# Order of the products over pairs of accumulator banks in a split-precision graph layer

## The chip, the cores and the metric

The kernel runs on one core of a Trainium2 chip. The metric is the device time of one launch in microseconds, from the core's own clock; lower is better. In the text PE is the engine for matrix products, PEld its weight loads, DVE the vector engine, ACT the scalar engine, POOL and SP two further engines that here only issue transfers.

## The reference

`x` and the item features are 10000 x 128, `adj` is 10000 x 10000, all in 32-bit floats.

```python
h_user = max(layernorm(x), 0)
h = item_feat @ W_item.T + b_item
b = h_user @ W_user.T + b_user
out = x + relu(adj @ h + b)
```

Nearly all of the work is `adj @ h`.

## The kernel before

The output is kept turned: 128 features by 10000 users. The users are cut into five groups (`GROUPS`) of 2048 columns, and a group into four accumulator banks (`ACC_BANKS`) of 512 columns; the last group's fourth bank has only 272. Two sets of four banks take turns from group to group. The 10000 items are cut into 78 chunks (`CHUNKS`) of 128, and 16 left over. A tile is one chunk of one group: 128 items by 2048 users of `adj`, 1 MB. There are 5 x 78 = 390 tiles, and the order is all chunks of group 0, then all of group 1, and so on.

Products run in a rounded 32-bit format. To keep precision, each operand is split in two: the rounded value (`hi`) and the remainder (`lo`). Three products stand for one: `h_lo` times the rounded columns (L799), `h_hi` times the rounded columns (L800) and `h_hi` times the remainder columns (L806). So a tile takes 4 banks x 3 products = 12 products, each with its own weight load.

A tile passes through the engines like this. SP loads it into `a_ring` (eight slots; `load_tile`, L273) when the tile eight before it has been used. ACT rounds it into `hi_ring` (four slots; `round_hi`, L382) when the tile four before it has been used. DVE subtracts and writes the remainder over the tile's own slot, seen as `lo_ring` (`subtract_lo`, L496). In the first two tiles of the first group both steps are made in quarters, and in the next ten in halves (`parts_of`, L390 and L505), so that PE can start sooner. The semaphores `part_hi` and `hi_written` tell of rounded columns, `part_lo` and `lo_written` of remainders. PE's `tile` tells with `chunk_used` (on the last bank's remainder product) that both slots of the tile are free, and in a group's last tile with `acc_done` that a bank is complete. DVE then empties the banks (`empty`, L633), behind the subtractions of the second and third tile of the next group.

Between tiles PE's program places small products: those that make `h` from the items (`h_trio`, L725, in the first group), the mean and the variance of the layer norm (L744, L750), the user products (L758; L766, L767 and L769 from the second group on) and those of the left-over items (L780). All queues are written out by hand and run in program order. The last two tiles of the last group are issued apart: first three banks of both (`over=range(PARTS)`), then the fourth of both.

Of the kernel before, what the change touches and what calls it, by code (L numbers as in the profile page):

```python
# [35 lines left out]
ACC_BANKS = 4  # L36
BANK_PITCH = 512
SLOT_W = ACC_BANKS * BANK_PITCH
BANK_W = 512
# [10 lines left out]
CHUNKS = N_ITEM // P  # L50
# [3 lines left out]
PAIR = 2  # L54
# [26 lines left out]
PARTS = ACC_BANKS - 1  # L81
# [25 lines left out]
def unit_at(c, at, every):  # L107
    k, rest = divmod(c - at, every)
    return k if rest == 0 and 0 <= k < UNITS else None


def at_of(g, step):
    return (FIRST if g == 0 else LATER)[step]


def bank_w(g, k):
    return LAST_BANK_W if g == GROUPS - 1 and k == ACC_BANKS - 1 else BANK_W
# [6 lines left out]
def parts_of(g, c):  # L124
    if g > 0 or c >= QUARTERED + HALVED:
        return 1
    return ACC_BANKS if c < QUARTERED else ACC_BANKS // 2


def parts_before(c):  # L130
    return sum(parts_of(0, i) - 1 for i in range(c))
# [6 lines left out]
def graph_layer(nc, adj_tiles, adj_rem, item_t, x_slices, x_t, mean_of, w_item_and_bias, w_user_t, b_user, out_t):  # L138
    with ExitStack() as ctx:
        def sb(name, shape, dt=F32):  # L140
            return ctx.enter_context(nc.sbuf_tensor(name, shape, dt))

        def sem(name):
            return ctx.enter_context(nc.semaphore(name))
# [9 lines left out]
        hi_ring = sb("hi_ring", [P, S_SLOTS, SLOT_W], F32R)  # L154
        h_hi = sb("h_hi", [P, CHUNKS, HID], F32R)
        h_lo = sb("h_lo", [P, CHUNKS, HID], F32R)
        ring_at = nc.sbuf_base
        a_ring = sb("a_ring", [P, A_SLOTS, SLOT_W])
        lo_ring = nc.alloc_sbuf_tensor_at("lo_ring", [P, A_SLOTS, SLOT_W], F32R, offset=ring_at)
# [27 lines left out]
        def acc_of(g):  # L187
            return banks[g % 2]
# [16 lines left out]
        part_hi = sem("part_hi")  # L205
        part_lo = sem("part_lo")
# [25 lines left out]
        hi_written = sem("hi_written")  # L232
        lo_written = sem("lo_written")
        chunk_used = [sem(f"chunk_used{s}") for s in range(S_SLOTS)]
        acc_done = sem("acc_done")
        y_ready = [sem(f"y_ready{k}") for k in range(ACC_BANKS)]
# [468 lines left out]
        def _(pe):  # L705
# [78 lines left out]
            def tile(g, c, over=range(ACC_BANKS)):  # L784
                n, acc = g * CHUNKS + c, acc_of(g)
                s, r = n % A_SLOTS, n % S_SLOTS
                parts = parts_of(g, c)
                for k in over:
                    part, within = divmod(k, ACC_BANKS // parts)
                    if within == 0 and part < parts - 1:  # L790
                        pe.wait_ge(part_hi, parts_before(c) + part + 1)
                    elif within == 0:
                        pe.wait_ge(hi_written, n + 1)
                    if c == 0 and g > 1:

                        pe.wait_ge(y_ready[k], g - 1)
                    cols = slice(k * BANK_W, k * BANK_W + bank_w(g, k))
                    hi, lo = hi_ring[:, r, cols], lo_ring[:, s, cols]
                    nc.tensor.matmul(acc[k][:, 0:bank_w(g, k)], h_lo[:, c, :], hi, start=(c == 0), stop=False, skip_group_check=True)  # L799
                    nc.tensor.matmul(acc[k][:, 0:bank_w(g, k)], h_hi[:, c, :], hi, start=False, stop=False, skip_group_check=True)  # L800
                    if within == 0 and part < parts - 1:
                        pe.wait_ge(part_lo, parts_before(c) + part + 1)
                    elif within == 0:

                        pe.wait_ge(lo_written, n + 1)
                    last = nc.tensor.matmul(acc[k][:, 0:bank_w(g, k)], h_hi[:, c, :], lo, start=False, stop=(c == CHUNKS - 1),  # L806
                                            skip_group_check=True)
                    if k == PARTS:
                        last.then_inc(chunk_used[r], 1)
                    elif c == CHUNKS - 1:  # L810
                        last.then_inc(acc_done, 1)

            pe.wait_ge(warm_set, 1)
            warm(WARM_FIRST)
# [3 lines left out]
            for g in range(GROUPS):  # L818
# [4 lines left out]
                for c in range(CHUNKS):  # L823
                    if g == 0:
                        if c == 1:
                            h_trio(1)
                        if c in (TRIO, TRIO + 1):
                            h_trio(c - 1)
                        if c % PIECE_TILES == 0 and PIECE_TILES <= c < (PIECES - 1) * PIECE_TILES:
                            for part in range(PIECE_TRIOS):  # L830
                                h_trio(c // TRIO + LEAD + part)
                        if c == H_REM_AT:
                            h_rem_product()
                    if c == at_of(g, "mean"):
                        mean_product(g)
                    if c == at_of(g, "var"):
                        variance_product(g)
                    k = unit_at(c, at_of(g, "user"), NORM_EVERY)
                    if k is not None and g == 0:
                        user_product(g, k)  # L840
                    elif k is not None:
                        user_parts(g, k)
                    if c == at_of(g, "rem"):
                        left_over(g)
                    if g == 0 and c == 0:
                        pe.wait_ge(h_first_lo_set, 1)
                    elif g == 0 and (c == 1 or c % TRIO == 0):

                        pe.wait_ge(h_lo_set, c // TRIO + 1)
                    if g < GROUPS - 1 or c < CHUNKS - 2:  # L850
                        tile(g, c)
            for c in (CHUNKS - 2, CHUNKS - 1):
                tile(GROUPS - 1, c, range(PARTS))
            for c in (CHUNKS - 2, CHUNKS - 1):
                tile(GROUPS - 1, c, range(PARTS, ACC_BANKS))
# [40 lines left out]
```

## Time and profile before

| | |
|---|---|
| time, median of 3 runs (lowest to highest) | 1091.58 us (1090.75 to 1091.82) |
| the profiled execution's own time | 1091.69 us |
| its span, first to last instruction | 1089.9 us |
| PE busy | 1084.3 us (99%) |
| weight loads busy | 900.4 us (83%) |
| DVE busy | 989.0 us (91%) |
| ACT busy | 776.3 us (71%) |
| granted clock of PE, mean | 1.000 |
| read from memory | 417.04 MB, 387 GB/s over the span |

Busy means that the engine has at least one instruction in flight. On PE the instructions overlap: one starts before the one before it has ended, and its end in the trace is modelled. So a PE that is 99% busy can still run at different rates, and what counts is the step from one start to the next. The difference of 1.8 us between the execution's time and its span lies before the first instruction and after the last.

### The profile page before, as it was taken

The numbers are of one execution on the slowest core, as the hardware profiler recorded it, in microseconds if no ns is written. First come the engines' busy times: TensorE is split into PE (matmuls) and PEld (weight loads), VectorE is DVE, ScalarE is ACT, GpSimd is POOL, SyncE is SP. The second block draws the span as 40 slices with busy tenths as digits, with TensorE's granted clock in tenths as the row PEclk, the third lists the DMA queues.
The fourth block names the chain that finished last, engine by engine and source line by source line (L and its number), as shares of the span: only waits on it lengthen the run. The fifth ranks groups of instructions, "written<-read, shape, count | busy, mean of one in ns | idle before, by whom it ended". The sixth has DMA issues, their size and how long they took to land.

```text
span 1089.9 us, 12124 instructions
## 1 busy us (share of the span) xinstructions
PE 1084.3 (99%) x4956; PEld 900.4 (83%) x4956; DVE 989.0 (91%) x640; ACT 776.3 (71%) x492; POOL 33.7 (3%) x67
## 2 busy tenths in 40 slices
PE   9999999999999999999999999999999999999998
PEld 8888888788888888888888888888888888888887
DVE  6989999999899998898999988989999889899986
ACT  6767777667777776677777766777777667777763
POOL 0000000000000000000000000000000000000000
PEclk9999999999999999999999999999999999999999
DMA  9999999999999999999999999999999999999993
GB/s 388 416 425 406 424 425 398 341 370 416 415 395 395 395 401 380 377 414 404 397 391 400 391 379 368 424 395 385 423 397 378 379 358 414 378 408 406 380 353 134
DMA packets 65194, 422.99 MB, mean 388 GB/s; under 512 B 7977, under 2 KB 8778, under 8 KB 25202
## 3 DMA queue, kind: packets, MB, share of 16 engines
q1 hardware_dynamic: 60386, 407.61, 93.3%
q0 software_dynamic: 4608, 14.46, 4.2%
q8 instruction: 39, 0.64, 0.2%
q14 instruction: 17, 0.14, 0.0%
q10 hardware_dynamic: 144, 0.13, 0.0%
HBM read 417.04 MB, written 5.12 MB: 387 GB/s over the span
## 4 chain that ended last, share of the span: by engine, by line
PE 95%; DMA 2%; DVE 2%; ACT 0%; issue 0%; DVEq 0%; SPq 0%
PE acc L799 31%; PE acc L806 31%; PE acc L800 31%; DMA a_ring<-in_adj_tiles 2%; PE acc L725 1%; DVE lo_ring L496 1%; DVE lo_ring L505 0%; PE acc L766 0%; PE acc L769 0%; PE acc L767 0%; PE acc L758 0%; PE acc L780 0%; ACT hi_ring L390 0%; ACT hi_ring L382 0%; DVE y L633 0%
## 5 line engine op out<-in xcount | busy, mean ns | idle before, releaser
L382 ACT CAST hi_ring<-a_ring 128x2048 fp32r<-128x2048 f32 (+1 forms) x378 | 708.3, 1874 | 288.7 <-PE acc L806 265.1
L496 DVE TENSOR_TENSOR lo_ring<-a_ring,hi_ring 128x2048 fp32r<-128x2048 f32 (+1 forms) x378 | 841.1, 2234 | 80.0 <-ACT hi_ring L382 77.5
L799 PE MATMUL acc<-hi_ring,h_lo 128*128 128x512 f32 (+1 forms) x1560 | 602.9, 387 | 0.0
L806 PE MATMUL acc<-lo_ring,h_hi 128*128 128x512 f32 (+1 forms) x1560 | 599.8, 385 | 0.3 <-DVE lo_ring L505 0.2
L800 PE MATMUL acc<-hi_ring,h_hi 128*128 128x512 f32 (+1 forms) x1560 | 599.8, 384 | 0.0
L806 PEld LDWEIGHTS acc<-lo_ring,h_hi 128*128 128x128 f32 x1560 | 292.8, 188 | 60.4 <-DVE lo_ring L505 1.3
L799 PEld LDWEIGHTS acc<-hi_ring,h_lo 128*128 128x128 f32 x1560 | 292.9, 188 | 59.7 <-issue 2.7
L800 PEld LDWEIGHTS acc<-hi_ring,h_hi 128*128 128x128 f32 x1560 | 292.9, 188 | 58.0 <-issue 0.7
L505 DVE TENSOR_TENSOR lo_ring<-a_ring,hi_ring 128x1024 fp32r<-128x1024 f32 (+1 forms) x28 | 28.7, 1064 | 2.8 <-ACT hi_ring L390 2.6
L390 ACT CAST hi_ring<-a_ring 128x1024 fp32r<-128x1024 f32 (+1 forms) x28 | 24.5, 926 | 7.1 <-DMA a_ring<-in_adj_tiles 7.0
L326 POOL DMA_DIRECT2D y<-in_x_t x20 | 10.8, 542 | 529.3 <-ACT hi_ring L382 529.3
L725 PEld LDWEIGHTS acc<-wi_bi,items 128*128 128x128 f32 x156 | 20.3, 197 | 1.1
L725 PE MATMUL acc<-wi_bi,items 128*128 128x128 f32 x156 | 20.5, 280 | 0.0
L323 POOL DMA_DIRECT2D rows<-in_x_slices x20 | 10.9, 543 | 276.1 <-DVE normed_t L622 215.4
L633 DVE SCALAR_TENSOR_TENSOR y<-acc,y 128x512 f32<-128x512 f32 (+1 forms) x20 | 12.7, 671 | 4.2 <-PE acc L806 3.8
L526 DVE TENSOR_TENSOR h_full<-acc,wi_bi 128x384 f32<-128x384 f32 x25 | 13.7, 550 | 2.7 <-PE acc L725 2.7
L622 DVE STREAM_TRANSPOSE normed_t<-rows 128x512 f32<-128x512 f32 (+1 forms) x20 | 14.0, 700 | 0.7
L403 ACT CAST h_hi<-h_full 128x384 fp32r<-128x384 f32 x25 | 12.7, 507 | 1.4 <-DVE h_full L526 1.4
L537 DVE TENSOR_TENSOR h_lo<-h_full,h_hi 128x384 fp32r<-128x384 f32 x25 | 13.7, 548 | 0.0
L615 DVE SCALAR_TENSOR_TENSOR rows<-rows,stat 128x512 f32<-128x512 f32 (+1 forms) x20 | 13.4, 671 | 0.0
L583 DVE TENSOR_TENSOR rows<-rows,acc 128x512 f32<-128x512 f32 (+1 forms) x20 | 13.3, 666 | 0.0
L575 DVE TENSOR_REDUCE stat<-rows 128x16 f32<-128x512 f32 (+1 forms) x20 | 13.3, 666 | 0.0
(55 smaller groups left out, 155.6 us busy)
## 6 DMA issues: line engine op xcount, KB each, us to landing
a_ring<-in_adj_tiles SPq DMA_DIRECT2D x312, 1024.0 KB, 7.4
a_ring<-in_adj_tiles SPq DMA_DIRECT2D x78, 904.0 KB, 6.6
rows<-in_x_slices POOLq DMA_DIRECT2D x19, 256.0 KB, 7.0
y<-in_x_t POOLq DMA_DIRECT2D x19, 256.0 KB, 6.8
items<-in_item_t SPq DMA_DIRECT2D x12, 384.0 KB, 11.3
out_t<-y POOLq DMA_DIRECT2D x16, 256.0 KB, 7.1
a_rem<-in_adj_rem SPq DMA_DIRECT2D x20, 100.0 KB
out_t<-y SPq DMA_DIRECT2D x3, 256.0 KB, 2.7
```

The costliest lines, as they stand in the source:

```text
L382: nc.scalar.copy(hi_ring[:, n % S_SLOTS, cols], a_ring[:, n % A_SLOTS, cols]).then_inc(hi_written, 1)
L390: nc.scalar.copy(hi_ring[:, r, cols], a_ring[:, s, cols]).then_inc(part_hi if part < parts - 1 else hi_written, 1)
L496: nc.vector.tensor_tensor(lo_ring[:, s, cols], a_ring[:, s, cols], hi_ring[:, r, cols], ALU.subtract).then_inc(lo_written, 1)
L505: nc.vector.tensor_tensor(lo_ring[:, s, cols], a_ring[:, s, cols], hi_ring[:, r, cols], ALU.subtract).then_inc(part_lo if part < parts - 1 ...
L526: nc.vector.tensor_tensor(h_full[:, trio % H_BANKS, :, :], h_banks[trio % H_BANKS][:, 0:TRIO_W].rearrange("p (c d) -> p c d", d=HID), bi.u ...
L537: nc.vector.tensor_tensor(h_lo[:, trio * TRIO:(trio + 1) * TRIO, :], h_full[:, trio % H_BANKS, :, :], h_hi[:, trio * TRIO:(trio + 1) * TRI ...
L615: nc.vector.scalar_tensor_tensor(out=rows[:, b, :], in0=rows[:, b, :], scalar=0.0, in1=inv[:, b].unsqueeze(2).broadcast_to(wide(b)), op0=A ...
L622: nc.vector.transpose(normed_t[:, 0:n, :], rows[:, b, :]).then_inc(normed_t_ready, 1)
L725: last = nc.tensor.matmul(out, items[:, slot, at:at + P], wi, start=(m == 0 or (trio, m) == (0, 1)), stop=True, skip_group_check=True)
L799: nc.tensor.matmul(acc[k][:, 0:bank_w(g, k)], h_lo[:, c, :], hi, start=(c == 0), stop=False, skip_group_check=True)
L800: nc.tensor.matmul(acc[k][:, 0:bank_w(g, k)], h_hi[:, c, :], hi, start=False, stop=False, skip_group_check=True)
L806: last = nc.tensor.matmul(acc[k][:, 0:bank_w(g, k)], h_hi[:, c, :], lo, start=False, stop=(c == CHUNKS - 1), skip_group_check=True)
```

## The change

Only PE's `tile` changes. In a tile that covers all four banks, the banks are taken as two pairs, (0, 1) and (2, 3). In each pair first come the two products with rounded columns of the one bank and then those of the other, then the remainder product of the one and that of the other. A tile's order of products was, with A for L799, B for L800, C for L806: A0 B0 C0 A1 B1 C1 A2 B2 C2 A3 B3 C3. It becomes A0 B0 A1 B1 C0 C1 A2 B2 A3 B3 C2 C3. The waits stay with the products that need them. The two last tiles of the last group, which are issued by parts, keep the old order.

```diff
--- before.py
+++ after.py
@@ -785,30 +785,35 @@
                 n, acc = g * CHUNKS + c, acc_of(g)
                 s, r = n % A_SLOTS, n % S_SLOTS
                 parts = parts_of(g, c)
-                for k in over:
-                    part, within = divmod(k, ACC_BANKS // parts)
-                    if within == 0 and part < parts - 1:
-                        pe.wait_ge(part_hi, parts_before(c) + part + 1)
-                    elif within == 0:
-                        pe.wait_ge(hi_written, n + 1)
-                    if c == 0 and g > 1:
-
-                        pe.wait_ge(y_ready[k], g - 1)
-                    cols = slice(k * BANK_W, k * BANK_W + bank_w(g, k))
-                    hi, lo = hi_ring[:, r, cols], lo_ring[:, s, cols]
-                    nc.tensor.matmul(acc[k][:, 0:bank_w(g, k)], h_lo[:, c, :], hi, start=(c == 0), stop=False, skip_group_check=True)
-                    nc.tensor.matmul(acc[k][:, 0:bank_w(g, k)], h_hi[:, c, :], hi, start=False, stop=False, skip_group_check=True)
-                    if within == 0 and part < parts - 1:
-                        pe.wait_ge(part_lo, parts_before(c) + part + 1)
-                    elif within == 0:
-
-                        pe.wait_ge(lo_written, n + 1)
-                    last = nc.tensor.matmul(acc[k][:, 0:bank_w(g, k)], h_hi[:, c, :], lo, start=False, stop=(c == CHUNKS - 1),
-                                            skip_group_check=True)
-                    if k == PARTS:
-                        last.then_inc(chunk_used[r], 1)
-                    elif c == CHUNKS - 1:
-                        last.then_inc(acc_done, 1)
+                for pair in (over if len(over) < ACC_BANKS else range(0, ACC_BANKS, PAIR)):
+                    of_pair = (pair,) if len(over) < ACC_BANKS else (pair, pair + 1)
+                    for k in of_pair:
+                        part, within = divmod(k, ACC_BANKS // parts)
+                        if within == 0 and part < parts - 1:
+                            pe.wait_ge(part_hi, parts_before(c) + part + 1)
+                        elif within == 0:
+                            pe.wait_ge(hi_written, n + 1)
+                        if c == 0 and g > 1:
+
+                            pe.wait_ge(y_ready[k], g - 1)
+                        cols = slice(k * BANK_W, k * BANK_W + bank_w(g, k))
+                        hi, out = hi_ring[:, r, cols], acc[k][:, 0:bank_w(g, k)]
+                        nc.tensor.matmul(out, h_lo[:, c, :], hi, start=(c == 0), stop=False, skip_group_check=True)
+                        nc.tensor.matmul(out, h_hi[:, c, :], hi, start=False, stop=False, skip_group_check=True)
+                    for k in of_pair:
+                        part, within = divmod(k, ACC_BANKS // parts)
+                        if within == 0 and part < parts - 1:
+                            pe.wait_ge(part_lo, parts_before(c) + part + 1)
+                        elif within == 0:
+
+                            pe.wait_ge(lo_written, n + 1)
+                        cols = slice(k * BANK_W, k * BANK_W + bank_w(g, k))
+                        last = nc.tensor.matmul(acc[k][:, 0:bank_w(g, k)], h_hi[:, c, :], lo_ring[:, s, cols], start=False,
+                                                stop=(c == CHUNKS - 1), skip_group_check=True)
+                        if k == PARTS:
+                            last.then_inc(chunk_used[r], 1)
+                        elif c == CHUNKS - 1:
+                            last.then_inc(acc_done, 1)
 
             pe.wait_ge(warm_set, 1)
             warm(WARM_FIRST)
```

## Rows read from the trace of the kernel before

**Rows 1.** The page: span, and busy us (share) x instructions of each engine.

```profile
span 1089.9 us, 12124 instructions
...
PE 1084.3 (99%) x4956; PEld 900.4 (83%) x4956; DVE 989.0 (91%) x640; ACT 776.3 (71%) x492; POOL 33.7 (3%) x67
```

**Rows 2.** Chain of work that ended last, whole span: share by line.

```profile
PE acc L799 31%; PE acc L806 31%; PE acc L800 31%; DMA a_ring<-in_adj_tiles 2%; PE acc L725 1%; DVE lo_ring L496 1%; DVE lo_ring L505 0%; PE acc L766 0%; PE acc L769 0%; PE acc L767 0%; PE acc L758 0%; PE acc L780 0%; ACT hi_ring L390 0%; ACT hi_ring L382 0%; DVE y L633 0%
```

**Rows 3.** Timeline of PE, undisturbed stretch: start us, us, engine, line, operation.

```profile
519.65 0.39 PE L806 MATMUL acc<-lo_ring,h_hi 128*128 128x512 f32 x1
519.88 0.39 PE L799 MATMUL acc<-hi_ring,h_lo 128*128 128x512 f32 x1
520.11 0.39 PE L800 MATMUL acc<-hi_ring,h_hi 128*128 128x512 f32 x1
...
560.00 0.39 PE L799 MATMUL acc<-hi_ring,h_lo 128*128 128x512 f32 x1
```

**Rows 4.** Groups by form: xcount | busy us, mean ns | idle before.

```profile
L799 PE MATMUL acc<-hi_ring,h_lo 128*128 128x512 f32 x1482 | 580.8, 392 | 0.0
```

**Rows 5.** Waits, whole span: who waited for whom, us, times, longest.

```profile
ACT hi_ring L382 <- PE acc L806: 265.1, 337, 3.5
...
PEld acc L806 <- DVE lo_ring L505: 1.3, 3, 0.6
...
PEld acc L806 <- DVE lo_ring L496: 0.5, 1, 0.5
```

**Rows 6.** Timeline of PE, first and third tile of the first group.

```profile
9.79 0.39 PE L800 MATMUL acc<-hi_ring,h_hi 128*128 128x512 f32 x1
...
10.12 0.50 PE L806 MATMUL acc<-lo_ring,h_hi 128*128 128x512 f32 x1
...
14.13 0.39 PE L800 MATMUL acc<-hi_ring,h_hi 128*128 128x512 f32 x1
...
14.70 0.50 PE L806 MATMUL acc<-lo_ring,h_hi 128*128 128x512 f32 x1 [0.17 <-DVE lo_ring L505]
...
15.03 0.40 PE L799 MATMUL acc<-hi_ring,h_lo 128*128 128x512 f32 x1
```

**Rows 7.** Timeline near 89.93: DVE's subtraction and the products of bank 0 and 1.

```profile
87.60 2.27 DVE L496 TENSOR_TENSOR lo_ring<-a_ring,hi_ring 128x2048 fp32r<-128x2048 f32 x1
...
89.45 0.39 PE L800 MATMUL acc<-hi_ring,h_hi 128*128 128x512 f32 x1
...
89.93 0.50 PE L806 MATMUL acc<-lo_ring,h_hi 128*128 128x512 f32 x1
...
90.26 0.39 PE L799 MATMUL acc<-hi_ring,h_lo 128*128 128x512 f32 x1
```

**Rows 8.** Timeline of PE, last group: narrow bank, then the next tile.

```profile
1077.81 0.28 PE L799 MATMUL acc<-hi_ring,h_lo 128*128 128x272 f32 x1
...
1077.93 0.30 PE L800 MATMUL acc<-hi_ring,h_hi 128*128 128x272 f32 x1
...
1078.07 0.29 PE L806 MATMUL acc<-lo_ring,h_hi 128*128 128x272 f32 x1
...
1078.19 0.39 PE L799 MATMUL acc<-hi_ring,h_lo 128*128 128x512 f32 x1
```

**Rows 9.** Timeline at the first change of group: bank 0's last product, L633.

```profile
241.01 0.39 PE L806 MATMUL acc<-lo_ring,h_hi 128*128 128x512 f32 x1
...
241.51 0.69 DVE L633 SCALAR_TENSOR_TENSOR y<-acc,y 128x512 f32<-128x512 f32 x1
```

**Rows 10.** Timeline of PE behind the mean product, and the user products of group 1.

```profile
428.40 0.40 PE L766 MATMUL acc<-turned_hi,wu_lo 128*128 128x512 f32 x1
...
429.11 0.39 PE L799 MATMUL acc<-hi_ring,h_lo 128*128 128x512 f32 x1
...
501.02 0.39 PE L800 MATMUL acc<-hi_ring,h_hi 128*128 128x512 f32 x1
...
502.88 0.39 PE L799 MATMUL acc<-hi_ring,h_lo 128*128 128x512 f32 x1
```

## The prediction, made before the changed kernel had run

> **What bounds the kernel now.** I read the busy shares first, then the chain of work that ended last, then the waits, and last the timeline at the few places where the product engine is late. The shares say that PE has work in flight for 1084.3 of 1089.9 us and DVE for 91% [rows 1]. The chain says which of the two matters: the three product lines of `tile`, L799, L800 and L806, carry 31% of the span each, and the transfer of the matrix and the whole tiles' subtraction 2% and 1% [rows 2]. So the time is a number of products times the step from the start of one to the start of the next.
>
> That step is the quantity to know. Durations of products do not give it, because each is shown at 0.39 us and overlaps the next. In an undisturbed stretch the same instruction, L799, starts at 519.88 and again at 560.00 us, with 177 products from the one to the other (59 of each of the three lines): 40.12 us by 177 is 226.7 ns [rows 3]. Such products, 512 columns wide, number 3 x 1482 = 4446 [rows 4]; times 226.7 ns that is 1007.9 us of the 1089.9. The three kinds of step also look alike: from L806 to the next bank's L799 it is 0.23 us, and from there to L800, in the same bank, 0.23 us again [rows 3]. The engines that feed PE wait for it rather than the reverse: ACT stands 265.1 us for L806, while PE's weight loads stand 1.3 us and 0.5 us for the subtraction in the whole run [rows 5].
>
> **What the change can touch.** It adds and removes no instruction: 12 products and 12 weight loads per tile stay, and so do all increments. It moves four things.
>
> *The wait for the remainders.* In a whole tile the first product that reads them (call it C0) was third and becomes fifth. PE now stands there in few places. In the third tile C0 would follow L800 of 14.13 at 14.36 and starts at 14.70, 0.34 us late; the step behind it is 0.33 instead of 0.23 us, since the next weights had not been loaded ahead. That is 0.44 us in all [rows 6]. Two more products ahead of it are 2 x 0.227 = 0.45 us, so this stall should just vanish. At 89.93 the same happens: due at 89.68, 0.25 us late, and 0.10 us for the refill, 0.35 us [rows 7]. The subtraction that it waits for began at 87.60 at the end of an unbroken row of DVE work behind a late transfer, and does not come earlier when PE does. PE comes there 0.44 us earlier by the first gain and has its C0 0.45 us further back in the tile, so it arrives at about 89.69 and still stands until 89.93; but only 7 products of the tile are then left rather than 9. The two gains do not add: at this point the kernel is 0.45 us ahead, whatever it had won before. If the transfers behind that stretch, which are issued when PE frees a slot, also land earlier, both add up to 0.44 + 0.35 = 0.79 us. I take 0.45, because the chain there runs through DVE and the transfer, not through PE.
>
> *The waits of the quartered first two tiles.* There bank 1's rounded columns are now waited for ahead of bank 0's remainder product. The end of such a tile is its last remainder product in both orders: that one stands at 10.12, a step of 0.33 us after the preceding product instead of 0.23, in both versions [rows 6]. I put 0 on it; a cost of up to one refill, 0.1 us, is the bound.
>
> *The narrow bank of the last group.* Its fourth bank has 272 columns in 78 tiles, 76 of which take the new order (the last two are issued apart and keep the old one). Now the steps behind its three products are 0.12, 0.14 and 0.12 us [rows 8]: the second product in a row is the slower one. In the new order the two rounded products still follow each other, and the narrow remainder product stands by itself between wide ones. If the third then has the step of a first one, the gain is nearly 0 (0.12 against 0.12); if the 0.14 was the price of the remainder product's place, up to 76 x 0.02 = 1.5 us. The row of the first narrow product after a wide one (0.12) is nearest for the isolated product, and the 0.14 stays with the pair; a rounding of 0.01 leaves some 4 ns, 76 x 4 ns = 0.3 us. I take 0.3 us, with 0 and 1.5 as ends.
>
> *What leaves later.* The slot release (`chunk_used`) rides on bank 3's remainder product, the twelfth of the tile in both orders, so ACT's casts and SP's loads, which wait for it, move by nothing. In a group's last tile `acc_done` of banks 0 and 2 comes two products, 0.45 us, later. DVE's L633 waits for it with all later subtractions queued behind. At the first change of group bank 0's last product starts at 241.01 with a duration of 0.39, and L633 at 241.51 [rows 9]: 0.11 us of air, so DVE would stand about 0.34 us. DVE is by the program text working two tiles ahead there (L633 comes behind the subtraction of the next group's second tile), and with 91% busy it has time to spare [rows 1], so this costs nothing; without that cover it would be 4 x 0.34 = 1.4 us. POOL's stores of `y` start as much later; what POOL does next, the loads of x, waits for the cast of the group's 14th tile anyway.
>
> The sum is 0.45 + 0.3 = 0.75 us. The profiled execution took 1091.69 us, 0.11 above the median of 1091.58, and its span 1089.9; taking the gain from the median gives 1090.8 us. Less than 0.2% (2.2 us), about what a measurement of this kernel can tell from no change, is "within".
>
> **Does the step itself depend on the order?** This is the large unknown, as 1 ns on all products is 4.4 us. Two things are new. Steps to another bank rise from one in three to four in six. In the trace steps to another bank and within a bank are both 0.23 us [rows 3], so this gives 0. The Trainium skill, "Perfetto Trace Analysis", Matmul Optimizations, says otherwise: "Ensure all 8 PSUM banks are being leveraged to maximize available instruction-level parallelism." The trace does not agree, as far as its two kinds of step go. The second: two products in six now have another weight load beside them. The remainder weights `h_lo` load beside a rounded product, and `h_hi` beside a remainder product. No row of before shows these two combinations settled. The three that it shows all have the same step, and none of them is told apart by chunk or slot, so I take no change, with the nearest disturbed rows as bounds (below). The Trainium skill, "TensorE: Matmul & The Clock Gate", Step-by-step, has the weight load on a read port of its own that doesn't slow the running product; by it this term is nothing too, though the slower steps of [rows 10] are not explained by it.
>
> **Rivals.**
> - *Within 0.2%, and nothing gained* (1091.6 us): the stall at 89.93 is only moved and the narrow bank takes 4 ns less in no place. It differs from my forecast by 0.75 us and its sign can't be told from it.
> - *Faster, start-up.* All that PE stands for the subtraction goes, 1.3 + 0.5 = 1.8 us [rows 5] and four refills of 0.1, and some 0.7 us come at the narrow bank: 2.9 us, 1088.7 us. Against it: the stall at 10.12 sits at a tile's last product [rows 6].
> - *Faster, banks.* Steps to another bank get shorter. From 272 to 512 columns the step grows from 0.121 (my reading of 0.12 [rows 8]) to 0.2267, 0.44 ns a column, so 512 columns need 225.5 and 1.2 ns is what a step has beyond its columns. Gone from all 4446 that is 5.3 us, 1085.5 us. It is against the equal steps in [rows 3].
> - *Slower, weight loads.* The two new combinations run like the steps behind a disturbance: 8 steps from 501.02 to 502.88 take 1.86 us, 232.5 ns each, though weights and columns are the usual ones; with `wu` as weights, three steps from 428.40 to 429.11 take 0.71 us, 237 ns [rows 10]. On 1482 products that is 1482 x 5.8 ns = 8.6 us, 1099.4 us, or 1482 x 10 ns = 14.8 us, 1105.6 us. It decides from (0.75 + 2.2) / 1482 = 2.0 ns per product. For it: the step is plainly sensitive to something beside its width. Against: in undisturbed stretches it returns to 226.7 by itself.
>
> **How the numbers follow.** The forecast's own case gets 0.62, nothing gained 0.14; both end within 0.2%, 0.76. Faster start-up 0.06 and banks 0.05 make 0.11. Slower weight loads get 0.13. The first two hold 1090 to 1092 us and not quite 8 in 10; the range reaches to the start-up rival with 1 us of scatter, 1087.5, and to half the price of the weight loads, 1090.8 + 4.3 = 1095.1, rounded to 1095.0, because they may strike one combination of the two only.
>
> **What would show it.** L799 to L799 across an undisturbed stretch after: 226.7 ns per product if right, 228.7 or more if the weight-load rival decides. The wait of L806's weight load for the subtraction: one entry left near 90 us, that at 14.7 gone. The narrow steps: 0.14 only behind the second of the rounded pair. The prediction is wrong if the settled step moves by even half a nanosecond on average.

## The result, and the profile after

The changed kernel takes 1093.61 us (1093.24 to 1093.96), the kernel before beside it 1091.12 us (1090.73 to 1092.22). The ratio is 1.0022, 95% interval 1.0015 to 1.0030: 2.5 us slower, where 0.75 us faster was forecast. The profiled execution took 1093.24 us, its span is 1091.4 us.

The page of the changed kernel answers to [rows 1] and [rows 2]. L799, L800 and L806 are now L801, L802 and L811.

```profile
span 1091.4 us, 12124 instructions
...
PE 1086.7 (100%) x4956; PEld 900.3 (82%) x4956; DVE 989.1 (91%) x640; ACT 776.1 (71%) x492; POOL 33.7 (3%) x67
...
PE acc L801 32%; PE acc L811 32%; PE acc L802 32%; PE acc L725 2%; PE acc L710 0%; PE acc L766 0%; PE acc L769 0%; PE acc L767 0%; PE acc L758 0%; PE acc L780 0%; DVE y L633 0%; PE acc L744 0%; PE acc L750 0%; DVEq L139 0%; PE acc L733 0%
```

The same instructions, the same products on the chain, and the transfer and the subtraction have left the chain: by the summary alone this kernel looks better. Only PE's time is 2.4 us longer. The table of waits (who waited for whom: us, times, longest) shows less waiting too, against 1.3 and 0.5 us in [rows 5]:

```profile
PEld acc L811 <- DVE lo_ring L505: 0.9, 3, 0.5
...
PEld acc L811 <- DVE lo_ring L496: 0.3, 1, 0.3
```

So no wait that the profile shows makes the loss. To find where it is, I laid the start of the same product in both timelines side by side: the first product of a group, and of tiles far apart. First groups 1 to 3, from their first product to that of the last group, kernel before (start us, us, engine, line, operation):

```profile
243.28 0.39 PE L799 MATMUL acc<-hi_ring,h_lo 128*128 128x512 f32 x1
...
892.76 0.39 PE L799 MATMUL acc<-hi_ring,h_lo 128*128 128x512 f32 x1
```

and the changed kernel:

```profile
242.40 0.39 PE L801 MATMUL acc<-hi_ring,h_lo 128*128 128x512 f32 x1
...
891.88 0.39 PE L801 MATMUL acc<-hi_ring,h_lo 128*128 128x512 f32 x1
```

Both take 649.48 us for 234 tiles. The order in pairs costs and brings nothing there. Now 67 tiles of the last group, kernel before:

```profile
912.12 0.39 PE L799 MATMUL acc<-hi_ring,h_lo 128*128 128x512 f32 x1
...
1078.19 0.39 PE L799 MATMUL acc<-hi_ring,h_lo 128*128 128x512 f32 x1
```

and the changed kernel:

```profile
911.55 0.40 PE L801 MATMUL acc<-hi_ring,h_lo 128*128 128x512 f32 x1
...
1080.24 0.39 PE L801 MATMUL acc<-hi_ring,h_lo 128*128 128x512 f32 x1
```

166.07 us against 168.69 us: 2.62 us in 67 tiles, 39 ns a tile. From the head of the last group (892.76 and 891.88) to those last rows it is 185.43 against 188.36 us, 2.93 us. The whole difference of the two spans, 1.5 us, is then -0.88 us up to the end of group 0 (0.18 of it because the first product happened to start earlier, at 7.015 instead of 7.197), 0.00 in groups 1 to 3, +2.93 us in the last up to its 76th tile, and -0.5 us behind that. This last part is no gain of the change: from the start of the last product to the end it is 3.99 instead of 4.58 us, and in the traces of all kernels of this document this stretch takes 3.93 to 4.67 us in either order. The medians, without the luck of single executions, say 2.5 us: 2.9 lost and about half a microsecond won.

One tile of the last group in the changed kernel (the rows "x2" are two products, C0 with C1 or C2 with C3):

```profile
921.41 0.40 PE L801 MATMUL acc<-hi_ring,h_lo 128*128 128x512 f32 x1
921.64 0.39 PE L802 MATMUL acc<-hi_ring,h_hi 128*128 128x512 f32 x1
921.87 0.40 PE L801 MATMUL acc<-hi_ring,h_lo 128*128 128x512 f32 x1
922.11 0.39 PE L802 MATMUL acc<-hi_ring,h_hi 128*128 128x512 f32 x1
922.34 0.62 PE L811 MATMUL acc<-lo_ring,h_hi 128*128 128x512 f32 x2
922.80 0.39 PE L801 MATMUL acc<-hi_ring,h_lo 128*128 128x512 f32 x1
923.03 0.39 PE L802 MATMUL acc<-hi_ring,h_hi 128*128 128x512 f32 x1
923.25 0.28 PE L801 MATMUL acc<-hi_ring,h_lo 128*128 128x272 f32 x1
923.38 0.30 PE L802 MATMUL acc<-hi_ring,h_hi 128*128 128x272 f32 x1
923.51 0.53 PE L811 MATMUL acc<-lo_ring,h_hi 128*128 128x512 f32 x2
923.87 0.39 PE L801 MATMUL acc<-hi_ring,h_lo 128*128 128x512 f32 x1
```

The six wide products from 921.41 to 922.80 take 1.39 us, 232 ns each; six settled ones take 1.36. Starts are rounded to 0.01 us here. The differences of neighbouring starts in the trace's own nanoseconds show it better. `w` is the step behind a wide product, `n` behind a narrow one; the stretch begins behind 930 us in both:

```
before:  121n 134n 125n 227w 226w 227w 227w 226w 227w 227w 226w 227w | 121n 134n 125n 227w ...
changed: 232w 125n 125n 238w 124n 234w 231w 236w 228w 233w 230w 227w 227w 121n 134n
         233w 131n 229w 233w 236w 224w 231w 236w 228w 233w 125n 125n 237w 125n 234w ...
means over 50 us:  before  226.7 wide, 126.7 narrow;  changed  231.5 wide, 126.7 narrow
```

The narrow products are not slower in the mean. The wide ones behind them are, by 4.8 ns, nine to a tile: 43 ns. Over all 67 tiles it is 39 ns, because the small products between some tiles disturb the wide ones of the kernel before as well, and the changed kernel loses less there than elsewhere (2548 against 2533 ns in the tile behind the mean product). And they run in a row of steps that the kernel before knows as well: behind the mean product it shows 229, 234, 235, 225, 230, 236, 229, 232, 231 and then 227 ([rows 10] have the start of the first and of the ninth of these steps, 501.02 and 502.88). There it is paid once in a while, here in every tile.

### The profile page after: what moved, and what is told of

It is laid out like the page before. It is cut to its first block, busy times and chain, and to the rows that moved or that the text cites. A ratio compares the mean times of both kernels' runs of the same rounds, so it can differ in the third digit from the quotient of the medians.

```text
span 1091.4 us, 12124 instructions
## 1 busy us (share of the span) xinstructions
PE 1086.7 (100%) x4956; PEld 900.3 (82%) x4956; DVE 989.1 (91%) x640; ACT 776.1 (71%) x492; POOL 33.7 (3%) x67
## 4 chain that ended last, share of the span: by engine, by line
PE 99%; DVE 0%; issue 0%; DVEq 0%; POOL 0%; POOLq 0%
PE acc L801 32%; PE acc L811 32%; PE acc L802 32%; PE acc L725 2%; PE acc L710 0%; PE acc L766 0%; PE acc L769 0%; PE acc L767 0%; PE acc L758 0%; PE acc L780 0%; DVE y L633 0%; PE acc L744 0%; PE acc L750 0%; DVEq L139 0%; PE acc L733 0%
## 5 line engine op out<-in xcount | busy, mean ns | idle before, releaser
L801 PE MATMUL acc<-hi_ring,h_lo 128*128 128x512 f32 (+1 forms) x1560 | 604.0, 387 | 0.0
L802 PE MATMUL acc<-hi_ring,h_hi 128*128 128x512 f32 (+1 forms) x1560 | 597.3, 385 | 0.0
L811 PE MATMUL acc<-lo_ring,h_hi 128*128 128x512 f32 (+1 forms) x1560 | 475.2, 385 | 0.0
L801 PEld LDWEIGHTS acc<-hi_ring,h_lo 128*128 128x128 f32 x1560 | 292.9, 188 | 64.0 <-issue 2.7
L802 PEld LDWEIGHTS acc<-hi_ring,h_hi 128*128 128x128 f32 x1560 | 293.0, 188 | 59.0 <-issue 0.7
L811 PEld LDWEIGHTS acc<-lo_ring,h_hi 128*128 128x128 f32 x1560 | 288.2, 188 | 56.9 <-DVE lo_ring L505 0.9
L633 DVE SCALAR_TENSOR_TENSOR y<-acc,y 128x512 f32<-128x512 f32 (+1 forms) x20 | 12.7, 671 | 4.9 <-PE acc L811 4.4
```

The costliest lines, as they stand in the source:

```text
L801: nc.tensor.matmul(out, h_lo[:, c, :], hi, start=(c == 0), stop=False, skip_group_check=True)
L802: nc.tensor.matmul(out, h_hi[:, c, :], hi, start=False, stop=False, skip_group_check=True)
```

## The experiments

Tile times below are (start of a product in the 76th tile of the last group less that in the 9th) / 67; before 166.07 us / 67 = 2479 ns, changed 168.69 us / 67 = 2518 ns. They hold the user products and the like too, which are equal in all. All kernels that are compared were timed beside the kernel before.

**Where the loss is: pairs in all groups but the last, and in the last alone.** In the changed kernel:

```diff
-                for pair in (over if len(over) < ACC_BANKS else range(0, ACC_BANKS, PAIR)):
-                    of_pair = (pair,) if len(over) < ACC_BANKS else (pair, pair + 1)
+                single = len(over) < ACC_BANKS or g == GROUPS - 1
+                for pair in (over if single else range(0, ACC_BANKS, PAIR)):
+                    of_pair = (pair,) if single else (pair, pair + 1)
```

and for the second kernel `g < GROUPS - 1` instead of `g == GROUPS - 1`.

> The order in pairs in groups 0 to 3, the old order in the last group. Theory A (the loss is made in the last group, by a narrow remainder product of 272 columns standing alone between wide ones): the start-up gain of 0.7 to 0.9 us stays and the 3.0 us of the last group (76 tiles of 40 ns) go, so 1091.1 - 0.8 = 1090.3 us, and a tile of the last group takes 2.42 us as before. Theory B (the last group is slow because of a state that the pairs of groups 0 to 3 leave behind, in the slots or the queues): a tile of the last group still takes 2.46 us, 1093.6 us.

> The order in pairs in the last group alone. Theory A: no start-up gain, the whole loss, 1091.1 + 3.0 = 1094.1 us, a tile of the last group 2.46 us. Theory B: 1091.1 us, 2.42 us a tile.

Measured: without pairs in the last group 1090.93 us, ratio 0.9997 (0.9988 to 1.0006), 2479 ns a tile. With pairs there only, 1094.50 us, ratio 1.0029 (1.0018 to 1.0039), 2518 ns a tile, beside 1091.25 us for the kernel before. The rows of the second, as far apart as those above, 168.69 us again:

```profile
912.24 0.40 PE L802 MATMUL acc<-hi_ring,h_lo 128*128 128x512 f32 x1
...
1080.93 0.39 PE L802 MATMUL acc<-hi_ring,h_lo 128*128 128x512 f32 x1
```

The loss belongs to the last group's own order. Nothing is carried over from the groups ahead: theory B falls. The time without pairs in the last group can't be told from that of the kernel before, as the interval holds 1; that the start-up gain is there is seen in the traces (below), not in this time.

**Which part of the order: a pair of wide banks alone, and a pair with the narrow products kept together.** First, in the last group:

```diff
-                for pair in (over if len(over) < ACC_BANKS else range(0, ACC_BANKS, PAIR)):
-                    of_pair = (pair,) if len(over) < ACC_BANKS else (pair, pair + 1)
+                pairs = [(k,) for k in over] if len(over) < ACC_BANKS else [(0, 1), (2,), (3,)] if g == GROUPS - 1 else [(0, 1), (2, 3)]
+                for of_pair in pairs:
```

> Pairs everywhere, but in the last group only banks 0 and 1 are a pair; banks 2 and 3 (the narrow one) are taken one after the other. Theory A: the three narrow products stand together again, no loss, 1090.3 us, 2.42 us a tile. Theory C (any pair in a tile with a narrow bank is slow, since its first products still run behind the narrow ones): half of the loss or more stays, 1091.8 to 1093.3 us, 2.44 to 2.46 us a tile.

Then the pair of banks 2 and 3 again, but with C3 ahead of C2:

```diff
-                    for k in of_pair:
+                    narrow_first = g == GROUPS - 1 and of_pair == (2, 3)
+                    for k in (of_pair[::-1] if narrow_first else of_pair):
...
-                        if k == PARTS:
+                        if k == (2 if narrow_first else PARTS):
```

> Pairs everywhere, but in the last group's second pair the narrow remainder product comes ahead of the wide one: A2 B2 A3 B3 C3 C2. The order in pairs stays and the three narrow products stand together. Theory A: 1090.3 us, 2.42 us a tile. Theory D (it is the pairing of a narrow bank with a wide one, not the lone product): 1093.6 us, 2.46 us a tile.

Measured: 1090.73 us and 2479 ns a tile for the first (ratio 0.9996, 0.9987 to 1.0005), 1091.31 us and 2481 ns a tile for the second (1.0000, 0.9991 to 1.0008). Two tiles of the second, from head to head:

```profile
1058.09 0.39 PE L801 MATMUL acc<-hi_ring,h_lo 128*128 128x512 f32 x1
...
1060.51 0.39 PE L801 MATMUL acc<-hi_ring,h_lo 128*128 128x512 f32 x1
...
1061.87 0.39 PE L801 MATMUL acc<-hi_ring,h_lo 128*128 128x512 f32 x1
1062.10 0.39 PE L802 MATMUL acc<-hi_ring,h_hi 128*128 128x512 f32 x1
1062.32 0.28 PE L801 MATMUL acc<-hi_ring,h_lo 128*128 128x272 f32 x1
1062.44 0.30 PE L802 MATMUL acc<-hi_ring,h_hi 128*128 128x272 f32 x1
1062.58 0.51 PE L812 MATMUL acc<-lo_ring,h_hi 128*128 128x272 f32 x2
1062.93 0.39 PE L801 MATMUL acc<-hi_ring,h_lo 128*128 128x512 f32 x1
```

Each is 2.42 us long, with pairs in it. One exchange of two neighbouring products, C2 and C3, takes 37 of the 39 ns away. It is that the three narrow products are split, and not the pair: theory C falls on the first kernel, theory D on the second.

**Does it need pairs at all?** The kernel before, with only the last group's order written out. Three orders were run, the first of them:

```diff
+                if g == GROUPS - 1 and len(over) == ACC_BANKS:
...
+                    for what, k in [('A', 0), ('B', 0), ('C', 0), ('A', 3), ('A', 1), ('B', 1), ('C', 1), ('B', 3), ('A', 2), ('B', 2), ('C', 2), ('C', 3)]:
```

> The kernel before, and in the last group the three narrow products each stand alone, three wide ones apart, with no pair of wide banks: A0 B0 C0 A3 A1 B1 C1 B3 A2 B2 C2 C3. Theory S: every wide product runs in the slow sequence, at least 3 x (2 + 7 + 8) = 51 ns a tile and the narrow steps on top, 2.47 to 2.50 us a tile, 1095 to 1097 us. Theory P (a pair of banks is needed for the loss, the order by itself does nothing): 1091.2 us.

Measured: 1094.82 us, ratio 1.0031 (1.0020 to 1.0042), 2526 ns a tile, 47 ns more than before. Theory S expected at least 51 ns more and 1095 us, so both lie just below its range; theory P falls. No banks are paired there, and the loss is larger than the change's. In the rows each wide bank's three products stand between two narrow ones (the row "x2" is a wide bank's remainder product and the narrow one behind it):

```profile
961.02 0.39 PE L799 MATMUL acc<-hi_ring,h_lo 128*128 128x512 f32 x1
961.25 0.40 PE L799 MATMUL acc<-hi_ring,h_hi 128*128 128x512 f32 x1
961.49 0.52 PE L799 MATMUL acc<-lo_ring,h_hi 128*128 128x512 f32 x2
961.84 0.40 PE L799 MATMUL acc<-hi_ring,h_lo 128*128 128x512 f32 x1
962.08 0.39 PE L799 MATMUL acc<-hi_ring,h_hi 128*128 128x512 f32 x1
962.31 0.40 PE L799 MATMUL acc<-lo_ring,h_hi 128*128 128x512 f32 x1
```

In nanoseconds the steps are `123n 228w 235w 234w 130n 230w 233w 236w 119n 234w 231w 233w`, a mean of 232.8 for the wide ones. The narrow ones are even shorter than before, 125.0 in the mean.

The other two differ from it in the list alone: `A3 A0 B0 C0 A1 B1 C1 A2 B2 C2 B3 C3` and `A3 B3 C3 A0 B0 C0 A1 B1 C1 A2 B2 C2`.

> The kernel before, and in the last group one narrow product (bank 3's first) moved to the head of the tile's line: A3 A0 B0 C0 A1 B1 C1 A2 B2 C2 B3 C3. C3 of the tile before still stands ahead of A3, so the narrow products stand as B3 C3 A3, three together across the border of two tiles. No pairs anywhere. Theory S (each departure of narrow products from three together makes the wide ones behind it run through the same slow sequence, 229, 234, 235, 225, 230, 236, 229, 232 ns, 40 ns in all, until they settle at 226.7): nothing lost, 1091.2 us, 2.42 us a tile. Theory T (it matters which of the three products stand together and how weights and tiles change there): 1093 to 1094.2 us.

> The kernel before, and in the last group the whole narrow bank ahead of the wide ones: A3 B3 C3 A0 B0 C0 and so on. Theory S: the three stay together, nothing lost, 1091.2 us, 2.42 us a tile. If the place in the tile counts (the wide bank 0 directly behind it): up to 1094 us.

Measured: 1092.08 us (1.0006, 0.9997 to 1.0015) and 2483 ns a tile for the first, and 1091.56 us (1.0000, 0.9991 to 1.0009) and 2479 ns for the second. The narrow bank may thus stand first in the tile as well as last. The first kernel shows more. Its first tile opens with A3 alone, with nothing narrow ahead of it. The first fifteen tiles of its last group then last 2.47 us each (without the mean product at the end of the fifteenth), though from the second on the three narrow products follow each other. Behind that product and one more tile they settle at 2.42 us, in the same order of products. One stretch from C3 to C3 of each kind:

```profile
904.82 0.29 PE L799 MATMUL acc<-lo_ring,h_hi 128*128 128x272 f32 x1
...
907.29 0.29 PE L799 MATMUL acc<-lo_ring,h_hi 128*128 128x272 f32 x1
...
934.58 0.30 PE L799 MATMUL acc<-lo_ring,h_hi 128*128 128x272 f32 x1
...
937.00 0.30 PE L799 MATMUL acc<-lo_ring,h_hi 128*128 128x272 f32 x1
```

In nanoseconds a tile has the steps `129n 238w 229w 234w 235w 225w 230w 236w 229w 232w 125n 125n` in the first stretch and `125n 227w 227w 226w 227w 227w 226w 227w 227w 226w 121n 134n` in the second. Fifteen times 47 ns is 0.70 us, and from the head of the group to its 76th tile this kernel takes 186.11 us against 185.43 before: 0.68 of the 1.0 us by which its median is higher. So three narrow products together cost nothing if the wide ones ahead of them have settled. If these still run in the slow row, the row can start anew behind them, tile after tile, as it did here until the mean product. Theory S holds only with this condition, and theory T falls, since the same three products stand together in both stretches.

**Is it the width?** In the kernel before and in the changed one the narrow bank was made wider, the further columns being zeros of padding:

```diff
-LAST_BANK_W = N_USER - (GROUPS * ACC_BANKS - 1) * BANK_W
+LAST_BANK_W = 480
```

> The kernel before with the last bank of the last group 480 columns wide in place of 272 (the further columns are zeros of padding). It is the reference for the next run: 78 x 3 products x 208 columns / 2.4 GHz = 20.3 us more than 1091.2, 1111.5 us, a tile of the last group 2.68 us.

> The changed kernel with the same 480 columns. Theory W (a lone narrow product disturbs because its step, 0.12 us, is shorter than the 0.19 us of a weight load, so that the load behind it comes late; at 480 columns the step is 0.21 us): no loss, 0.7 us under the run with the old order, 1110.8 us. Theory N (any change of width inside a tile disturbs the following products, whatever the width): 3 us lost and 0.7 won, 1113.8 us. Theory F (only a width that is no multiple of 32 disturbs): no loss, 1110.8 us.

> The kernel before with 384 columns in that bank: 78 x 3 x 112 columns / 2.4 GHz = 10.9 us more than 1091.2, 1102.1 us, a tile of the last group 2.56 us. Reference for the next run.

> The changed kernel with 384 columns. The step is 0.17 us, shorter than a weight load of 0.19 us. Theory W: a loss of 1 to 3 us against 0.7 won, 1102.4 to 1104.4 us. Theory N: the whole 3 us, 1104.4 us. Theory F: no loss, 1101.4 us.

| columns | old order, us | pairs, us | old order, ns a tile | pairs, ns a tile |
|---|---|---|---|---|
| 272 | 1091.12 | 1093.61 | 2479 | 2518 |
| 384 | 1104.93 | 1105.82 | 2657 | 2669 |
| 480 | 1115.19 | 1115.01 | 2792 | 2791 |

All three theories fall on the old order, which was only meant as a reference. It should have been 1102.1 and 1111.5 us and is 2.8 and 3.7 us slower. Its wide steps are no longer settled: at 384 columns `171n 175n 178n 240w 225w 230w 236w 229w 232w 231w 227w 226w` in every tile, at 480 `213n 221n 213n 235w 233w 236w 224w 231w 236w 228w 232w 231w`. That is the same slow row, entered at another of its members. "Settled" means here steps of 226.7 ns again. So three narrow products together are neutral at 272 columns, but not by being together: at other widths the old order is already disturbed, and pairs add 12 ns (384) or nothing (480). Taken as a difference, 0.9 us more at 384 columns would have fitted theory W, and 0.2 less at 480 has the sign that it named, though it put 0.7 less. But it has nothing to say on the disturbed old order at 480 columns, where no step (213 ns and more) is shorter than a weight load (0.19 us).

Three more widths in the old order, each run once, asked whether a bound in width divides the two cases. The edit is the same with 288, 256 and 336. With 256 the last 16 users are left out.

> The kernel before with 288 columns in the narrow bank. Undisturbed, a tile of the last group takes 9 x 226.7 + 3 x (288 + 32) / 2.4 = 2440 ns. Theory G (three narrow products together are neutral only because 272 happens to bring the row back to its settled rhythm): at 288 some wide steps of 229 to 240 ns stand in every tile, 2.45 to 2.49 us. Theory H (three together are neutral below some width between 272 and 384): 2.44 us and all wide steps at 226.7 ns.

> The kernel before with 256 columns in the narrow bank (the last 16 users are left out). Undisturbed 9 x 226.7 + 3 x (256 + 32) / 2.4 = 2400 ns a tile. Theory G: 2.41 to 2.45 us. Theory H: 2.40 us.

> The kernel before with 336 columns in the narrow bank. Undisturbed 9 x 226.7 + 3 x (336 + 32) / 2.4 = 2500 ns a tile. Theory G: 2.51 to 2.55 us, wide steps of 229 to 240 ns. Theory H, with its bound above 336: 2.50 us; with the bound below, as theory G.

Measured 1093.24, 1091.04 and 1100.66 us, beside 1091.16 for the kernel before, all single times. The steps repeated in every tile are `128n 132n 130n 233w 233w 231w 226w ...` at 288, `113n 120n 120n 233w 236w 228w 233w 230w 227w ...` at 256, and `150n 155n 157n 233w 233w 236w 224w 231w 236w 228w 233w 231w` at 336. The timeline of 256 columns:

```profile
959.91 0.28 PE L799 MATMUL acc<-hi_ring,h_lo 128*128 128x256 f32 x1
...
960.26 0.40 PE L799 MATMUL acc<-hi_ring,h_lo 128*128 128x512 f32 x1
960.49 0.40 PE L800 MATMUL acc<-hi_ring,h_hi 128*128 128x512 f32 x1
960.73 0.39 PE L806 MATMUL acc<-lo_ring,h_hi 128*128 128x512 f32 x1
...
962.33 0.28 PE L799 MATMUL acc<-hi_ring,h_lo 128*128 128x256 f32 x1
```

A tile lasts 2.42 us, as long as with 272 columns, though it has 48 columns less in its three narrow products: what their steps save (353 instead of 380 ns) the wide ones behind them give back. In the group's first tile, behind a settled group 3, it lasted 2393 ns. Both neighbours of 272 and all wider ones tried are disturbed. Against the sums worked out ahead of the runs the tile is 20, 7, 47, 40 and 53 ns longer at 256, 288, 336, 384 and 480 columns. Theory H falls, G stands: of the widths tried, 272 in threes is the one that leaves settled wide products in their rhythm. Theory G names what is seen and not its cause.

**How much of the start-up is to be had.** In the first group all four banks' rounded products first, pairs in groups 1 to 3, old order in the last:

```diff
-                for pair in (over if len(over) < ACC_BANKS else range(0, ACC_BANKS, PAIR)):
-                    of_pair = (pair,) if len(over) < ACC_BANKS else (pair, pair + 1)
+                pairs = [(k,) for k in over] if len(over) < ACC_BANKS else [(k,) for k in over] if g == GROUPS - 1 else [(0, 1, 2, 3)] if g == 0 else [(0, 1), (2, 3)]
+                for of_pair in pairs:
```

> In the first group all four banks' products with rounded columns come first (eight) and then the four remainder products; pairs in groups 1 to 3, the old order in the last group. If the start-up gain comes from how far back the first remainder product stands: what still stands near 89.5 us (0.1 us for a refill) goes too, 1090.6 us, and the stall at the end of the first tile stays since it is at the tile's last product. If the longer row of products costs by itself in a whole group: 1091 us or more.

Measured 1090.57 us, ratio 0.9993 (0.9984 to 1.0002): it is 3 us faster than the changed kernel and can't be told from the one before. The stretch from the first product to the head of the fourth tile is 10.00 us, to that of the 29th tile 84.68 us. With pairs in the first group it is 10.04 and 84.83 in the changed kernel and 10.03 and 84.71 in that with pairs in all groups but the last. With the old order it is 10.48 to 10.61 and 85.17 to 85.54 us in ten traces. One trace with pairs (480 columns) shows 10.62 and 85.30, so an execution can also miss the gain. Having eight rounded products ahead instead of four thus brings next to nothing more in the traces. Nor is the gain clear of the interval in the time of any kernel; it rests on the traces.

## Why the prediction was wrong

**The narrow bank: the step that failed.** I took the 76 tiles' narrow products by their own steps only, and put 0.3 us of gain on them with bounds of 0 and 1.5, so that a loss was not in the term at all. The narrow products do keep their sum: 126.7 ns in the mean in both kernels. The sign that I named, 0.14 us behind the second rounded one alone, is seen in every second tile (121, 134 and 131 ns); the others have 125, 125 and 124. The price is paid by the nine wide products behind them, 39 ns a tile and 2.93 us in the group. What was missing from the sum was a row for what a narrow product does to its followers. I had it in hand: [rows 10] show 232.5 ns on eight wide products behind a product of another width. I used it as the price of the weight-load rival, on products that had nothing narrow before them, and did not ask what had set those eight off. Put on the nine wide products of 76 tiles, the row's 5.8 ns would have given 4.0 us; 4.8 ns were measured in an undisturbed stretch and 39 / 9 = 4.3 ns over the 67 tiles.

**The weight-load rival** forecast the right sign by the wrong mechanism. Its two new combinations occur in groups 1 to 3 just as often per wide tile, and these are equal to 0.01 us in 649.48. Its size per product was about right (5.8 against 4.8 ns) and its place was wrong.

**The bank rival** falls on the same rows. Steps to another bank went from one in three to four in six and nothing moved: 226.7 ns stays. The trace of before had it right. The rule of the Trainium skill ("Perfetto Trace Analysis", Matmul Optimizations) that all eight banks are to be used is kept by both kernels, two sets of four; that changing banks more often would shorten the step was read into it, and these traces don't bear it out.

**The waits: right in the sum, and in part by luck.** PE's stall at 14.70 us is gone, worth 0.44 us by the sum; the weight load still waits a little (the row at 14.52 below), but the product behind it starts on time. The old order has 10.48 to 10.61 us to the fourth tile, the pairs 10.02 to 10.04 in all but one trace, 0.5 us between the medians. Near 90 us I argued that the two gains don't add, since DVE's subtraction would not come earlier. In the changed kernel's trace it began at 87.16 instead of 87.60 [rows 7]:

```profile
14.52 0.30 PEld L811 LDWEIGHTS acc<-lo_ring,h_hi 128*128 128x128 f32 x2 [0.19 <-DVE lo_ring L505]
...
87.16 2.27 DVE L496 TENSOR_TENSOR lo_ring<-a_ring,hi_ring 128x2048 fp32r<-128x2048 f32 x1
...
89.48 0.30 PEld L811 LDWEIGHTS acc<-lo_ring,h_hi 128*128 128x128 f32 x2 [0.25 <-DVE lo_ring L496]
```

Counted from the first product that is 80.14 instead of 80.41, and the old order alone has 79.80 to 80.41 in its ten traces, so this says nothing of the change. The stall itself varies as much: the tile in which it stands, the 28th, takes 3.13 us at the least, and in the ten traces of the old order it takes 0.00 to 0.38 us more, 0.07 in the median. The 0.35 us that I read from one trace was close to the worst case, and there was little to win. By the medians of the traces the start-up gain to the 29th tile is 85.25 - 84.73 = 0.5 us, against 0.45 in the sum: nearly all of it is the first stall. The quartered tiles cost nothing that could be seen, as put.

**What leaves later** cost nothing, as put: DVE stood once more for L811 ahead of L633, 0.52 us at the first change of group where I had put 0.34 (4.4 us in two times instead of 3.8 in one, the rest being the end of the last group), and groups 1 to 3 did not feel it.

**The range** reached to 1095.0 and held the time, but for a reason that the kernel did not have. The measured 2.5 us lie just beyond the 0.2% (2.2 us) to which I gave a chance of 0.76. That chance rested on two rows of one undisturbed stretch in a group whose products are all alike, and was carried over to the group in which they are not.

## What to carry to other kernels

When products of unlike width share a queue, price a reordering by the steps of the products behind the odd one, not by the odd one itself, and take them from a stretch of the very group in which it stands. The cheap remedy is to keep the order there and change it elsewhere: pairs everywhere but in the group with the narrow bank took 1090.9 us, against 1093.6. Compared with the kernel before, beside it 1091.25, that is no gain that the times can tell. A narrower bank need not be faster: 16 columns less took as long as 272 (one run each). 16 more took 2.1 us more, of which the columns alone account for 1.6 (78 x 3 x 16 / 2.4 GHz, an estimate). And look at more than one stretch of a group: the same order can run through it in two ways, 2.42 or 2.47 us a tile, by the state in which it was entered.

## What the runs showed of the hardware

A row of equal products of 512 columns, each with its own weight load, settles at a step of 226.7 ns, at a granted clock of 1.00. After small products or a narrow one it mostly does not return at once but runs through a fixed row of steps, `229 234 235 225 230 236 229 232 231` or, without its first member, `233 236 224 231 236 228 233 231`, the same within 1 ns in all traces. From its head to its end it costs about 40 ns. Where it is entered depends on the widths passed and on whether the products ahead had settled. From a settled row 272 columns three times skip it, and 256, 288, 336, 384 and 480 three times don't. From within the row 272 columns three times led back into it in fifteen tiles of one kernel. A tile with 256 columns takes as long as one with 272. The Trainium skill, "TensorE: Matmul & The Clock Gate", Back-to-back issue gap, gives about 216 ns for an isolated product of 512 columns, by a formula in its own width, and about 131 ns for a sustained stream of products with weight loads. These traces show neither: 226.7 ns settled, and 224 to 240 by what went before. Which two things in the engine get out of step here no run tells; that it isn't the bank, nor the pairing, nor the narrow bank's place in the tile, they do.
